# Shared-key attention: the order of maxima units and value products within a step

## The reference, cut to what matters

```python
q = (x @ Wq).reshape(Bsz, Tlen, H, D)
k = x @ Wk
v = x @ Wv
scores = jnp.einsum('bihd,bjd->bhij', q, k) / jnp.sqrt(jnp.float32(D))
scores = jnp.where(causal, scores, -jnp.inf)
attn = jax.nn.softmax(scores, axis=-1)
out = jnp.einsum('bhij,bjd->bihd', attn, v).reshape(Bsz, Tlen, C)
return out @ Wo + bo
```

## Time and profile before

| | |
|---|---|
| median of 3 runs | 1589.44 us (1588.42 to 1589.71) |
| the profiled execution's own time | 1589.51 us |
| its span, first to last instruction | 1587.7 us |
| TensorE busy over the span | 95% |
| VectorE, ScalarE, POOL busy | 65%, 49%, 23% |
| mean granted TensorE clock | 0.99 |
| the attention's units, first to last | 187 to 586 us |
| its value products, first to last | 211 to 646 us |

### The profile page before, as it was taken

How to read it: one execution, slowest core, us unless ns; L and a number is a source line. 1 busy time by engine, 2 the same in 40 slices (tenths; PEclk the granted TensorE clock), 3 DMA queues, 4 the chain that set the end, 5 groups by cost and what they waited for, 6 DMA issues and landing times.

```text
span 1587.7 us, 35631 instructions
## 1 busy us (share of the span) xinstructions
PE 1509.0 (95%) x14908; PEld 944.1 (59%) x14908; DVE 1033.7 (65%) x1866; ACT 780.5 (49%) x1801; POOL 362.7 (23%) x404
## 2 busy tenths in 40 slices
PE   7999889999999999899999989999999999999998
PEld 4667455444444444445666647777777777764556
DVE  4678678888898875624436965367787778842223
ACT  2431447777768887231111254377767677641110
POOL 2322000001000004100000044344555555630000
PEclk9999889999999999999999999999999999999999
DMA  6000231000000003100000040000000020000000
GB/s 195 2 2 8 80 87 21 13 10 10 14 3 14 3 13 116 61 2 19 1 0 0 1 133 1 7 1 8 1 8 1 1 91 1 2 0 1 14 14 27
DMA packets 31822, 39.05 MB, mean 25 GB/s; under 512 B 7531, under 2 KB 26606, under 8 KB 31150
## 3 DMA queue, kind: packets, MB, share of 16 engines
q1 hardware_dynamic: 31662, 36.77, 8.0%
HBM read 23.79 MB, written 2.10 MB: 16 GB/s over the span
## 4 chain that ended last, share of the span: by engine, by line
PE 80%; DVE 12%; ACT 3%; issue 3%; POOL 1%; DMA 0%; SPq 0%; POOLq 0%; ACTq 0%; DVEq 0%
PE PS L1264 7%; PE PS L1494 7%; PE PS L1500 7%; PE PS L1219 7%; PE PS L1523 7%; PE PS L2743 6%; PE PS L1250 6%; DVE arena L1403 4%; PE PS L2250 4%; PE PS L2730 3%; PE PS L2708 3%; PE PS L2573 2%; PE PS L340 2%; PE PS L2220 2%; PE PS L2589 2%
## 5 line engine op out<-in xcount | busy, mean ns | idle before, releaser
L1333 ACT ACTIVATE arena<-PS 128x512 f32<-128x512 f32 (+3 forms) x640 | 313.7, 534 | 119.7 <-PE PS L1254 57.5
L1403 DVE TENSOR_REDUCE arena<-PS 128x1 f32<-128x1024 f32 (+7 forms) x320 | 326.8, 1059 | 56.5 <-PE PS L1222 40.6
L1250 PE MATMUL PS<-arena 99*32 99x512 bf16 (+3 forms) x2560 | 210.8, 350 | 1.4 <-ACT arena L1333 1.0
L1219 PE MATMUL PS<-arena 96*32 96x512 bf16 (+3 forms) x2560 | 184.2, 356 | 18.1 <-DVE arena L1403 17.1
L1264 PE MATMUL PS<-arena 128*32 128x512 f32 (+3 forms) x1280 | 148.2, 536 | 2.2 <-ACT arena L1339 1.4
L191 POOL TENSOR_TENSOR rstd<-ve,mhalf 128x4 f32<-128x4 f32 x31 | 31.7, 1022 | 503.7 <-DVE ve L219 503.6
L2894 ACT ACTIVATE arena<-arena 128x128 f32<-128x128 f32 x256 | 122.7, 485 | 0.0
L1494 PE MATMUL PS<-XT,arena 128*128 128x512 f32 x256 | 120.4, 592 | 0.9 <-DVE arena L1731 0.9
L2743 PE MATMUL PS<-arena 128*128 128x256 f32 x512 | 121.0, 379 | 0.2
L1500 PE MATMUL PS<-XT,arena 128*128 128x512 f32 x256 | 120.3, 592 | 0.0
L1219 PEld LDWEIGHTS PS<-arena 96*32 96x32 bf16 x2560 | 64.1, 98 | 94.2 <-DVE arena L1403 42.8
(11 more groups left out here) (251 smaller groups left out, 2694.7 us busy)
## 6 DMA issues: line engine op xcount, KB each, us to landing
arena<-arena SPq DMA_DIRECT2D x79, 128.0 KB, 2.4
XT<-in_L_attn_xT SPq DMA_DIRECT2D x4, 512.0 KB, 7.4
X<-in_L_attn_x SPq DMA_DIRECT2D x4, 512.0 KB, 9.3
arena<-in_L_attn_out_w SPq DMA_DIRECT2D x1, 2048.0 KB, 8.2
out<-X SPq DMA_DIRECT2D x3, 512.0 KB, 3.0
arena<-in_dmask SPq DMA_DIRECT2D x1, 1024.0 KB, 5.7
arena<-in_L_ffn_W_up SPq DMA_DIRECT2D x1, 1024.0 KB, 5.1
arena<-in_L_ffn_W_gate SPq DMA_DIRECT2D x1, 1024.0 KB, 7.5
```

The costliest lines, as they stand in the source:

```text
L1219: last = pe.matmul(flat[p, o:o + w], q[:, p], a.KS[0:SROWS, CH * kc:CH * kc + w], start=True, stop=kc < c)
L1250: last = pe.matmul(PS[p, b, lo:CH], keys[:, p], a.QS[0:rows, G1 * g + r, CH * c + lo:CH * (c + 1)], start=True, stop=j < TPC * c)
L1333: act.activation(a.PB[:, n % 3, r, lo:CH], PS[:, 4 + x % 3, lo:CH], ACT.Exp, scale=D0 ** -0.5).then_inc(a.e2, 1)
L1403: dve.tensor_reduce(dst, src, AX.X, ALU.max, negate=True).then_inc(a.m1, 1)
```

## The change

Within a step the second part of the units is issued ahead of the third score, and the value product between the third and the fourth. The order was: score 0, units, score 1, value product, score 2, units, score 3. It is then: score 0, units, score 1, units, score 2, value product, score 3. The programs of the other engines are as they were.

```diff
--- before.py
+++ after.py
@@ -1295,12 +1295,12 @@
             unit(u)
         if scored:
             score(n + 1, 1)
+        for u in units[half:]:
+            unit(u)
+        if scored:
+            score(n + 1, 2)
         if 0 <= n < P1.nb:
             value(n)
-        if scored:
-            score(n + 1, 2)
-        for u in units[half:]:
-            unit(u)
         if scored:
             score(n + 1, 3)
         if n in P1.out_at:
```

## The result

The kernel after takes 1582.78 us (median of 4 runs, 1580.62 to 1584.33), beside 1588.93 us for the kernel before on the same chip (4 runs, 1588.42 to 1589.71). The ratio is 0.9959 (0.9945 to 0.9973), so 6.2 us or 0.41% are gained. The forecast was 1586.5 with a range of 1582 to 1591: it has the right side, and less than half of the gain. The profiled execution of the kernel after is the slowest of its four, at 1584.33. Ahead of the stage the two profiled executions differ by what the clock granted early on (over the first 100 us 1.00 before and 0.98 after; the first unit starts at 186.97 and 188.61, the first value product at 211.44 and 213.32; the steps put at most 0.7 of this last 1.9 there). Therefore I compare stretches of the stage, and never absolute times.

A forecast was written before the change was run, and what follows sets the result against it. TensorE, busy for 95% of the span, was taken as the bound, with waits in some steps. Terms -3.5 - 1.0 - 0.8 - 0.9 + 2.7 + 0.5 + 0.1 = -2.9 us, from 1589.44 to 1586.5; range 1582 to 1591.

The forecast's parts named there:

- The three-unit stretch: Steps of three units, 300 to 330 us: the third unit waits for the first one's pair of banks; +2.7 us.
- the wait at 219: TensorE's 1.32 us wait behind two splits on VectorE shrinks, as the reduction ahead comes earlier; -0.8 us.
- the steps after the last unit: Exponentials bound there; with the third score ahead of the value product ScalarE runs through, 2.24 us a step; -0.9 us.
- the clock of a pair: From a unit's start to the freeing of its pair of banks by VectorE's reduction: 1.93 us.
- -3.5 at transposes: Steps with a maxima transpose: the first unit's wait for the previous step's last reduction goes; -3.5 us.
- -1.0 at group ends: Where a group of heads ends: the value product's wait for ScalarE's bank copy fits, narrow steps lose some; -1.0 us.
- Plain steps: 0: Two-unit steps without transpose or group end: no new wait, still 2.63 us each; change 0.
- The second three-unit stretch: Three-unit steps alternating with two-unit ones, 425 to 463 us: 39.2 us against 38.7; +0.5 us.
- Four units: Four-unit steps, 225 to 246 us: four steps lose 0.4 to 0.6, the two after get it back; +0.1 us.
- The full stretches lose nothing: Rival, chance 0.22: three- and four-unit steps cost nothing as VectorE runs nearly without gaps; gains alone, 1583.3 us.
- The waits only move: Rival, chance 0.16: each wait removed at a transpose returns at the second unit of the same step; 1589.4 us.
- Slower by the detour: Rival, chance 0.12: VectorE starves 0.87 us in each full step, 1599 us; or the clock halves there, 1601.

The follow-up runs named there:

- swap alone: Against the kernel before, only the value product and the third score change places; the second part of the units stays behind both: 1584.33 us, ratio 0.9968.
- units alone: Against the kernel before, only the second part of the units moves, ahead of the value product; the third score stays behind that product: 1587.17 us, ratio 0.9987.
- spread only: Against the kernel before, units of three- and four-unit steps are issued singly between scores and value product; other steps keep the old order: 1586.21 us, ratio 0.9982.
- at transposes: Against the kernel before, only the ten two-unit steps ahead of a maxima transpose get the changed order: 1585.35 us, ratio 0.9970.

## Why the prediction was right, and where its sizes were off

**Right, term by term.** The three-unit stretch (+2.63 for +2.7, V(34) 3.80 for 3.82), the wait at 219 (-0.77 for -0.8), the steps after the last unit (-0.98 for -0.9, 2.24 each), the clock of a pair (1.93), and the worth of later gains at the end (none; the wait for VectorE grew instead). Four of the five hold as they were worked out, instruction by instruction from rows. The one at 219 is partly luck: the wait itself shrank by 0.55 only (1.32 to 0.77), and from first score to first score 0.43 of the stretch's gain stand in step 4, which begins with a transpose that the forecast had no term for. The experiments confirm who pays: the old order put back in the full steps returns 5.0 us of trace, and the swap by itself carries all of the gain after the last unit.

**The term that was mis-sized most: two-unit steps, -9.22 for -4.5.** The prediction had -3.5 at transposes, -1.0 at group ends, and 0 in "Plain steps: 0". Taken by whole periods of one `i`, from a plain step to a plain step, so that V's place drops out:

| steps | before, us | after | forecast | more than forecast |
|---|---|---|---|---|
| 24 to 32, chunk 1 | 20.18 | -0.86 | -0.46 | -0.40 |
| 48 to 60, chunk 2 | 31.81 | -1.37 | -0.96 | -0.41 |
| 60 to 72, chunk 2 | 31.31 | -1.29 | -0.96 | -0.33 |
| 96 to 112, chunk 3 | 41.19 | -0.92 | -0.31 | -0.61 |
| 112 to 128, chunk 3 | 41.19 | -0.95 | -0.31 | -0.64 |

Where the excess stands can be read from first score to first score, over the 106 steps of the two-unit stretches, sorted by kind, and for the two moves by themselves:

| kind of step | steps | after, change | forecast | swap alone | units alone |
|---|---|---|---|---|---|
| with a transpose, and the one ahead of it | 18 | -5.7 | -3.5 | 0.0 | -5.1 |
| three narrow steps at a group's end | 27 | +2.4 | | -0.15 | +2.1 |
| first step behind them | 9 | -4.0 | | -1.6 | -1.8 |
| (the last two together) | | -1.65 | -1.0 | | |
| plain | 52 | -1.6 | 0 | -0.7 | -0.8 |

So half of the excess stands at the transposes, and it is a wrong size in the working: by it U1 could go at 366.54, when the score's mask is through. That is 0.44 behind the score's own start. Timeline of PE before, that start:

```profile
366.10 0.34 PE L1250 MATMUL PS<-arena 99*32 99x384 bf16 x3
```

After, the score starts at 366.56. A score, and each half of a unit, is four matmuls, one for each 32 of the output's partitions (a column tile). Three of the unit's start already at 366.80, 0.24 behind the score's start, while the score's fourth, begun at 366.72, is still running. So U1 comes 0.92 sooner behind its score (1.16 before, from 366.10 to 367.26), and not 0.72. At group ends the forecast has "chunk 3 nothing"; the swap alone gains 0.37 or 0.38 in each such period, 0.22 of it at the group's end.

Then there is a gain of 0.03 in a plain step, 2.60 for the 2.63 that the forecast wanted to see unchanged. Most of it is V's own 0.02, which the waits show. View of waits, steps of the stage, before (for what the engine waited: total us, times, longest):

```profile
PEld PS L1264 <- ACT arena L1333: 19.1, 60, 0.6
PEld PS L1264 <- ACT arena L1339: 5.8, 10, 0.7
```

and what is left of it after:

```profile
PEld PS L1264 <- ACT arena L1339: 0.2, 1, 0.2
```

Before, V's weights weren't loaded until the exponential that V waits for was done, in 60 steps, and TensorE began V with its weights still to come. After, V comes late enough for them to be loaded ahead. In the plain step, timelines of PEld before and after:

```profile
488.52 0.16 PEld L1264 LDWEIGHTS PS<-arena 128*32 128x32 f32 x8 [0.33 <-ACT arena L1333]
...
487.16 0.34 PEld L1264 LDWEIGHTS PS<-arena 128*32 128x32 f32 x8
```

The first stands at V's own start (488.52), the second 0.21 ahead of it (487.37). V's eight matmuls take 0.88 us before and 0.86 after. In the profiles the two go together: the mean length of a line 1264 matmul is 535 or 536 ns in the three kernels in which V comes straight behind S1 in two-unit steps (before, spread only, at transposes), and 528 or 529 in the seven others. One of these is units alone, where V is still ahead of S2, but with a unit between S1 and V; its weight loads wait for an exponential 10 times and 3.2 us. So it is V's lateness that counts, and either move gives it. But each move by itself gives a part back elsewhere: in fourteen like plain steps (98 to 104 and 114 to 120) the step lasts 2.656 us before, 2.642 with the swap alone, where the two scores that now follow each other take 0.452 instead of 0.444, 2.640 with the units alone, where the first unit takes 0.443 instead of 0.434, and 2.625 after. That the weight loads are the cause of V's 0.02 is argued from this, and not tested by itself. The prediction looked for waits of TensorE's matmuls alone and not for those of its weight loads. It wrote of the swap that S2 "loses nothing by going first", which is true, and stopped there: it didn't ask what V gains by going later.

**Two smaller ones.** *The second three-unit stretch* cost +1.03 for +0.5, and nearly all of the error is one step: V(82) to V(83) took 3.52 for the 3.00 of the list, while the eleven others came within 0.11. Timelines of PE and DVE after in that step:

```profile
439.48 0.51 PE L1219 MATMUL PS<-arena 96*32 96x512 bf16 x8 [0.63 <-DVE arena L1403]
```

```profile
437.88 0.68 DVE L1419 TENSOR_TENSOR arena<-arena 128x512 f32<-128x512 f32 x1
438.48 4.16 DVE L1403 TENSOR_REDUCE arena<-PS 128x1 f32<-128x768 f32 x4
```

The product of a finished pair of groups (line 1419) runs on VectorE between the reductions that the third unit waits for. I had left it out of the working. *Four units* cost +0.83 for +0.1: the four full steps took 3.81, 3.99, 4.54, 5.05 for 3.52, 3.97, 4.43, 5.06, and the last step 2.04 for 1.75. The first and the last make 0.6 of it; I haven't taken them apart further.

**The rivals.** *The full stretches lose nothing* gave 1583.3, which is near the measured time, and it is wrong: they lose 4.5 us (0.83 + 2.63 + 1.03), and the gains are 10.7 instead of 6.2. A total alone would have crowned the wrong story; only the stretches tell it apart. *The waits only move* is in part true of a kernel that was not the change: it is what happens to some of the gain when only single units go early. The change itself has some of it as well, the 2.4 us that the narrow steps of nine groups lose, 0.26 a group, where the forecast had counted waits of 0.25 to 0.5. *Slower by the detour* was worked out with 18 full steps, and there are 20. With 20 it needed 6.2 / 20 = 0.31 us in each to decide; they lose 4.5 / 20 = 0.23, and 3.3 / 20 = 0.17 had been counted. Its other half, the clock, didn't come: the windows above stand at 1.00 with a wait of 0.6 or more in the steps shown. The rule on short idle times between groups that cycle through PSUM banks (the Trainium skill, "TensorE: Matmul & The Clock Gate", section "A second HAM failure mode: psum-queue depth-cycling") doesn't show in this trace, whose three-unit steps of 3.8 us hold such waits.

**Open** is why the two moves together gain 1 us more than apart, of which 0.6 stand at the transposes (-5.7 for -5.1 and 0.0), and why two scores back to back, or a unit ahead of them, take the 0.01 more. By their runs' intervals the two sums can't be told apart.

## What to carry to other kernels

With two buffers taken in turn, what counts is the distance from a producer to its next use of the same buffer, over the whole train: moving one producer early moves a part of its wait to the one before, and grouping two of three makes the third wait until the first has made its full pass (1.93 us from start to start here), so spread the producers evenly and move all of them. Where two operations need the same signal, put first the one that fills another engine's queue; and read the waits of the weight loads beside those of the matmuls. Compare a change stretch by stretch, because gains of 11 us and losses of 4.5 in one total look like a small gain from one cause.

## What the runs showed of the hardware that wasn't expected

- The transposes of the maxima are nearly free beside column-tiled matmuls. They are 12 columns wide: in the rows around 366.50 three quarters of the next score start at 366.56, 0.06 after the first transpose, and only the fourth waits until 366.72. The prediction charged 0.22 for them.
- Late weights go with only 0.02 us more in a group of eight f32 matmuls of 512 columns (0.88 for 0.86), although the weight load's wait is 0.3 us long in the row (19.1 / 60).
- Idle times of TensorE of 5.15 us in 33, in pieces like the 0.62 shown, left the granted clock at 1.00 in the kernel after. At the end of the stage it fell to 0.50 (1.2 of 2.4 GHz) in the windows 639 to 645 after and 645 to 651 before; in front of it TensorE had waited 1.99 and 1.42 us for the last turn. At transposes had the same wait of 1.42 there and stayed at 1.00, so that the wait alone doesn't decide it.
